# VectorE's gate multiply between two Newton steps of a reciprocal root, in the first stage of a gated two-layer kernel

## The reference

```python
h   = layernorm(x)                       # (x - mean) / sqrt(var + 1e-5)
g   = silu(h @ C_e.T);  u = h @ C_e.T    # the same product
x1  = x + tanh(g_xattn) * ((g * u) @ C_e.T)
xh  = layernorm(x1)
out = x1 + tanh(g_ffn) * (routed(xh) + shared(xh))
```

## Time and profile before

| | |
|---|---|
| median of 3 runs | 479.32 us (479.09 to 480.01) |
| the profiled execution's own time | 480.27 us |
| its span, first to last instruction | 478.5 us |
| TensorE busy / weight loads busy | 460.1 us (96%) / 392.7 us (82%) |
| VectorE busy | 328.6 us (69%) |
| ScalarE busy | 255.4 us (53%) |
| GpSimd busy | 211.1 us (44%) |
| granted clock of TensorE, mean | 0.995 of full speed |

### The profile page before, as it was taken

One profiled execution on the slowest core, in us unless ns is written; L12 is line 12 of the kernel. 1 busy time (PEld: TensorE's weight loads), 2 busy tenths in 40 slices (PEclk: granted clock), 3 DMA queues, 4 the chain that ended last, 5 costly groups with the idle time before them and its releaser, 6 DMA issues.

```text
span 478.5 us, 7813 instructions
## 1 busy us (share of the span) xinstructions
PE 460.1 (96%) x2493; PEld 392.7 (82%) x2493; DVE 328.6 (69%) x724; ACT 255.4 (53%) x379; POOL 211.1 (44%) x175
## 2 busy tenths in 40 slices
PE   2999999999999999999999999999999999999993
PEld 1477778888888888888888999999999999999992
DVE  6689899998987844488559776676666666667520
ACT  4764445545553543542436575656655676666531
POOL 0513444565443475435177445434525545542242
PEclk9999999999999999999999999999999999999998
DMA  7643656876665443363379999989869998887555
GB/s 298 187 174 125 198 179 201 292 258 226 206 214 175 175 121 114 86 79 46 43 198 185 296 294 264 267 279 272 266 193 263 254 267 269 264 248 226 110 63 70
DMA packets 30460, 95.02 MB, mean 199 GB/s; under 512 B 4960, under 2 KB 7008, under 8 KB 29920
## 3 DMA queue, kind: packets, MB, share of 16 engines
q0 software_dynamic: 17040, 43.66, 37.3%
q1 hardware_dynamic: 13104, 50.98, 31.2%
q10 hardware_dynamic: 288, 0.01, 0.0%
HBM read 67.50 MB, written 28.70 MB: 201 GB/s over the span
## 4 chain that ended last, share of the span: by engine, by line
PE 91%; DVE 3%; DMA 2%; ACT 1%; issue 1%; POOL 0%; POOLq 0%; DVEq 0%
PE psG L1291 49%; PE psY L1291 30%; PE psT L1296 7%; PE psG L1549 1%; DMA out<-xh_sb,idx 1%; PE psG L1320 1%; DMA tok_i<-in_ids 1%; PE psY L1308 1%; ACT arena L571 0%; POOLq L81 0%; ACT arena L562 0%; PE psY L1427 0%; PE psG L1321 0%; POOL out L521 0%; ACT front L583 0%
## 5 line engine op out<-in xcount | busy, mean ns | idle before, releaser
L1291 PE MATMUL psY<-arena 128*128 (+1 forms) x372 | 91.0, 394 | 0.4 <-DVE arena L921 0.4
L1291 PEld LDWEIGHTS psY<-arena 128*128 128x128 f32 x372 | 68.8, 188 | 14.8 <-issue 0.8
L512 POOL DMA_INDIRECT ht<-out,idx x32 | 33.6, 1051 | 64.6 <-PE psT L1296 48.8
L1291 PE MATMUL psY<-slot,arena 128*128 128x512 f32 x240 | 59.0, 395 | 0.0
L1066 DVE TENSOR_TENSOR slot<-raw,slot 128x1536 fp32r<-128x1536 f32 x25 | 43.9, 1760 | 19.7 <-ACT slot L638 19.6
L1291 PE MATMUL psG<-arena 128*128 x228 | 57.0, 398 | 0.0
L1066 DVE TENSOR_TENSOR arena<-raw,arena 128x1536 fp32r<-128x1536 f32 x24 | 42.0, 1756 | 16.6 <-ACT arena L638 16.4
L1291 PEld LDWEIGHTS psY<-slot,arena 128*128 128x128 f32 x240 | 44.2, 188 | 9.5 <-ACT xh_sb L682 0.3
L1291 PE MATMUL psG<-arena,slot 128*128 128x512 f32 x216 | 51.3, 392 | 0.0
L1291 PEld LDWEIGHTS psG<-arena 128*128 128x128 f32 x228 | 41.5, 188 | 8.5 <-issue 0.4
L1291 PEld LDWEIGHTS psG<-arena,slot 128*128 128x128 f32 x216 | 40.1, 188 | 8.2
(11 more groups left out here) (228 smaller groups left out, 803.9 us busy)
## 6 DMA issues: line engine op xcount, KB each, us to landing
raw<-in_w SPq DMA_DIRECT2D x48, 768.0 KB, 5.6
padded<-xh_sb SPq DMA_DIRECT2D x19, 256.0 KB, 2.2
raw<-in_w SPq DMA_DIRECT2D x12, 192.0 KB, 4.3
raw<-in_ctx_t SPq DMA_DIRECT2D x2, 1024.0 KB, 8.7
ht<-in_ctx_t SPq DMA_DIRECT2D x1, 1024.0 KB, 11.7
xh_sb<-in_ctx_t SPq DMA_DIRECT2D x1, 1024.0 KB, 9.5
out<-log_sb SPq DMA_DIRECT2D x4, 256.0 KB, 8.2
ht<-out,idx POOLq DMA_INDIRECT x32, 4.5
```

Source lines behind the costliest of these rows:

```text
L512: pool.indirect_dma_start(ht[:, n, :], None, halves_of_out, slots(e * NA + a, 0)).then_inc(g_here[n], 16)
L1291: ins = pe.matmul(ps, left[a], right[b], start=n == 0 and m == 0, stop=n == total - 1 and m == 2)
```

## The change

The gate multiply of steps 1 to 18 is taken from its place behind the root and put into the middle of it, behind the last instruction of the first Newton step (L983) and ahead of the second Newton step. Its two waits (for silu and for the transposes of the tile before) move with it. In step 0 it stays where it was, at the head of the step. In all of steps 1 to 18 the root runs, so each has exactly one gate multiply, as before. The low half of h (`low_h`) stays behind L993.

```diff
@@ -983,6 +983,8 @@
                             nw(dve.scalar_tensor_tensor(Y, T, -((27 / 4 * RS_W) ** (1 / 3)), Y, ALU.add, ALU.mult))
                             if pair:
                                 low_h()
+                            if have(known, 0) and known > 0:
+                                gate1()
                     nw(dve.scalar_tensor_tensor(T, T, -10 / 3 * RS_W, T, ALU.add, ALU.mult))
                     if had(known, 2):
                         dve.wait_ge(h_ready, t + 2)
@@ -991,8 +993,6 @@
                     nw(dve.scalar_tensor_tensor(R, T, 5 * RS_W ** 2, Y, ALU.add, ALU.mult))
                     assert n[0] == NEWTON
                     dve.scalar_tensor_tensor(B, mv[:, cs, 0], -1.0, R, ALU.mult, ALU.mult).then_inc(norm_ready, 2 if pair else 1)
-                if have(known, 0) and known != 0:
-                    gate1()
                 if have(known, 1) and known not in (FIRST + 1, 0):
                     low_h()
                 if pair:
```

## The result

The changed kernel takes 484.36 us (median of 6 runs, 483.3 to 484.51) against 479.18 us (6 runs, 478.66 to 480.01): a ratio of 1.0097, 95% interval 1.0085 to 1.0108. It is slower, as forecast, but by 0.8 us more than the upper end of the range. The difference of the medians is 5.2 us where 2.8 was forecast. The profiled executions lie closer together: 484.42 us (span 482.4) after, 480.27 us (span 478.5) before, 4.15 us and 3.9 us of span. Why these two differences are not the same is most of what follows.

A forecast was written before the change was run, and what follows sets the result against it. TensorE, 91% of the chain, was taken to bound the kernel. Its delays in the first stage summed to 3.2 us, cut to 2.8 for a shorter landing: 479.3 + 2.8 = 482.1 us, range 479.6 to 483.6.

The forecast's parts named there:

- What bounds the kernel, and what comes behind the gate: First stage: TensorE bounds; the norm replaces the gate as limit of the h transposes, 0.27 us per step where TensorE waits.
- Step 1: The gate waits for silu until 32.12 us, L925 moves from 32.99 to 33.60, VectorE 0.61 us late.
- Steps 3 and 5: L993 of step 3 1.22 us late, the scatter's landing shifts equally, h transposes of step 5 1.49 us late.
- Steps 6 to 11: Mostly waits for silu make the h transposes later: 1.80 us in step 7, 2.70 in step 9, +2.9 at the end.
- Steps 12 to 16: Steps 12 to 15, with four more transposes each, add nothing; step 16 adds 0.3 us.
- the last of the sum: Step 5: with a landing of some 5.3 us L916 wouldn't wait, 0.44 us less lost; 2.8 taken instead of 3.2.
- (a): TensorE's four waits for the gate go, 2.5 us won, 476.8 us; chance 0.06.
- (b): The landing stays in place, VectorE's slack hides losses of steps 6 to 11; some 0.6 us lost, 479.9 us; chance 0.14.
- (c): The loop through the DMA dominates, loss grows in all of steps 6 to 11; 4 us or more, 483.5 us; chance 0.15.
- The bound: Upper end: landings 0.5 us longer, step 5 and two later turns adding about as much each, +4.3 us.

The follow-up runs named there:

- a_nolock: The changed kernel with L976 and L977 given two input tiles instead of one; 484.13 us, 1.0084 of the kernel before.
- b_again: The kernel before, run again without an edit for a second profile; 479.62 us, ratio 0.9991.
- m5_11: The kernel before with the gate moved in steps 5 to 11 alone; 482.49 us, 1.0046 of the kernel before.

## Why the prediction was wrong in size, and which of its steps failed

**What bounds the kernel, and what comes behind the gate.** Right. TensorE's waits for the gate shrink and the norm takes their place. L995 stands 1.38 us behind the gate (forecast 1.40), the h transposes 1.06 us behind L995 (1.13).

**Step 1.** Right: the gate starts at 32.13, L925 at 33.58 (forecast 32.12 and 33.60). A gate that waits starts 0.09 us behind silu here, not 0.03.

**Steps 3 and 5.** Right for the profiled executions: the coefficients at 48.03 (48.04), L916 of step 5 at 57.85 (57.73), h transposes at 64.55 (64.51).

**Steps 6 to 11.** The h transposes come as forecast in step 7 (77.94, forecast 77.99) and step 9 (91.77, forecast 91.69), but not quite for the reason given. The forecast let silu hold the gate in steps 7 and 8; in the trace the chain holds it, 0.19 us behind L983 (75.49 where silu had ended at 75.38, 82.31 where it had ended at 82.00), because L977 is long in both (0.35 and 0.36 us). Without that, silu and the chain would let the gate start within 0.2 us of each other in both steps (an estimate from these rows), so it is partly luck that the figure of step 7 fits to 0.05 us. Steps 10 and 11 were said to end at +2.9 and ended at +3.38. The missing 0.5 us is the waits of L976 and L977 for GpSimd, 0.18 to 0.24 us in each of steps 7 to 11 where the kernel before has one, and with them L916 of step 11, which started at 99.00; a_nolock, without the long ones, has these h transposes 0.67 us earlier. Nothing in the forecast had a term for two engines that hold each other up; the row of 0.41 us was in the trace of before and I took the duration of a chained instruction for a constant.

**Steps 12 to 16.** Right: no loss in 12 to 15, and +0.3 from step 16 (3.38 to 3.67).

**The step that failed** is the last of the sum: "with a landing of some 5.3 L916 of step 5 wouldn't wait for it ... so 0.44 less is lost". I saw that the landing of 6.94 us was not the usual one of the kernel before, which b_again and three others of its order bear out. I then took it as chance for both kernels. It isn't chance for the changed one. The landing is long when the scatter of step 3 meets TensorE's instruction packet, the old order stands within 0.1 us of the edge, and the change takes 0.5 us off the distance (4.5 to 4.0), over the edge in all three traces with its order on VectorE and GpSimd and the packet in place. An execution of the changed kernel therefore has the whole wait of L916 in step 5, 1.8 us (57.85 against the 56.06 at which VectorE is free), and four of six traces with the old order up to step 4 have none of it. For a median execution without the wait the correction had to go up by 1.15 us, what L916 waits in the first trace of before, and I took it down by 0.44. The sum in the profiled executions was short too: 3.2 us where the spans differ by 3.9, mostly by the 0.5 us of steps 10 and 11. With 3.9 us and 1.15 (the two profiled executions of before, 480.27 and 479.13, lie 1.14 apart), 5.05 of the 5.2 us of the medians is accounted for. That the median execution of before is one without the wait is inferred from these traces, not measured.

**The rivals.** (a), the gates win, has nothing for it. (b), the early steps anchored and the later ones hidden by VectorE's slack, fell with m5_11. (c), the loop over the DMA, was nearer than its 0.15: it binds in step 5 and in step 7 (L916 at 71.40, behind a landing at 71.20), and its 483.5 us is still below the time measured. The bound allowed for landings 0.5 us longer; a scatter that meets the packet lands 1.1 to 2.1 us later (6.5 to 7.2 us against 5.1 to 5.4).

## What to carry to other kernels

When an instruction is moved ahead in a chain, ask what the chain's end releases before what the moved one releases. Here one engine waited for the gate by 2.5 us in all, and a norm, a gather, a scatter and its landing hung on the end that was pushed back. A duration that is far from its group's median in one trace is a question with two answers, chance or an edge; if it is an edge, the change may put every execution on the wrong side of it. And of a chain of small instructions, look at the longest as well as at the mean: the few long ones show what another engine does to it.

## What the runs showed of the hardware that I had not expected

- A 16 KB packet of TensorE's instruction stream took 0.97 us in the changed kernel, and the transfer of 256 KB that was in flight in step 3 landed 1.1 to 2.1 us later where the two met (6.5 to 7.2 us against 5.1 to 5.4): the last 1.3 us of it were eight 4 KB packets in a row, at a DMA share of one engine. In step 8 a scatter at the same distance from such a packet was not delayed (4.9 us). 36 tiny matmuls with their weight loads at TensorE's start moved the packet from 54.6 to 46.0 us; with 96 empty ones nothing moved and no record of them is in the trace.
- A VectorE operation of 128 x 2 elements with one input tile takes 0.17 us alone and up to 0.42 us beside a GpSimd instruction that issues an indirect DMA, to whose end it waits if it starts 0.54 us or more behind that one's start. One that starts earlier passes (L976 at 101.92 in the changed kernel, 0.17 us, inside GpSimd's 101.58 to 102.55). The same work with two input tiles took 0.16 us there. Why the first 0.54 us are free isn't shown.
